# Wavelet mixer and gated feed-forward: sums of x and beta ahead of the weights, weights behind 1/den, the wait for zero pads at its reader

## The reference

```python
for _ in range(2):                                    # two analysis levels
    l = dwconv(low, h_filter)[:, ::2]
    h = dwconv(low, g_filter)[:, ::2]
    highs.append(h); low = l
low = linear_attention(low, 16)                       # q = k = elu(x) + 1, v = x, num / den
for h, L in zip(reversed(highs), reversed(lens)):     # two synthesis levels
    low = dwconv(repeat(low, 2), h_synth) + dwconv(repeat(h, 2), g_synth)
x = layernorm(x + (layer_norm(x + low) * gamma + beta))
gate, up = x @ wg.T, x @ wu.T                         # hidden width 1536, weights are integers / 127
x = layernorm(x + (silu(gate) * up) @ wd.T)
```

## Time and profile before

| | us |
|---|---|
| median of 3 runs | 1240.98 |
| lowest and highest | 1240.42, 1242.96 |
| the profiled execution | 1242.78 |
| its span | 1241.0 |

### The profile page before, as it was taken

One profiled execution on the slowest core, in us unless ns is written; L12 is line 12 of the kernel. 1 busy time (PEld: TensorE's weight loads), 2 busy tenths in 40 slices (PEclk: granted clock), 3 DMA queues, 4 the chain that ended last, 5 costly groups with the idle time before them and its releaser, 6 DMA issues.

```text
span 1241.0 us, 18461 instructions
## 1 busy us (share of the span) xinstructions
PE 1200.7 (97%) x5936; PEld 629.8 (51%) x5936; DVE 983.6 (79%) x1917; ACT 674.4 (54%) x1395; POOL 381.7 (31%) x794
## 2 busy tenths in 40 slices
PE   7968799999999999999999999999999999999997
PEld 6857454444544454444544544454445454454443
DVE  7968699998899989997799669965998579844231
ACT  5851474568545774567535653476355653565332
POOL 0013443146230652145221533044313522152201
PEclk9998899999999999999999999999999999999999
DMA  6794341203202221213102121212120210010000
GB/s 225 233 239 77 114 143 35 102 26 134 89 18 94 69 85 36 102 35 111 44 12 100 60 61 35 94 51 69 34 102 19 93 43 18 26 60 1 9 26 34
DMA packets 51864, 91.79 MB, mean 74 GB/s; under 512 B 8896, under 2 KB 28608, under 8 KB 50880
## 3 DMA queue, kind: packets, MB, share of 16 engines
q1 hardware_dynamic: 50048, 86.01, 21.3%
q0 software_dynamic: 1728, 4.72, 2.0%
HBM read 65.99 MB, written 25.19 MB: 73 GB/s over the span
## 4 chain that ended last, share of the span: by engine, by line
PE 81%; DVE 3%; POOL 3%; ACT 2%; issue 2%; POOLq 0%; DVEq 0%; ACTq 0%
PE ps_up L610 13%; PE ps_up L611 12%; PE ps_gate L610 12%; PE ps_gate L611 12%; PE ps_down L629 12%; PE ps_down L628 12%; PE ps_y L593 2%; PE ps_x L575 2%; PE ps_x L554 1%; PE ps_down L779 1%; POOL rs L1138 1%; DVE h L1211 1%; DVE l L1211 0%; DVE h_f L1599 0%; PE ps_x L534 0%
## 5 line engine op out<-in xcount | busy, mean ns | idle before, releaser
L610 PE MATMUL ps_gate<-x_hi,w 128*128 128x512 f16 x768 | 292.0, 380 | 1.6 <-DVE x_lo L1392 1.6
L610 PE MATMUL ps_up<-x_hi,w 128*128 128x512 f16 x768 | 291.9, 380 | 0.8 <-DVE h_f L1599 0.8
L611 PE MATMUL ps_gate<-x_lo,w 128*128 128x512 f16 x768 | 292.1, 380 | 0.0
L611 PE MATMUL ps_up<-x_lo,w 128*128 128x512 f16 x768 | 291.7, 380 | 0.0
L629 PE MATMUL ps_down<-w,hid 128*128 128x512 f16 x768 | 291.1, 379 | 0.0
L628 PE MATMUL ps_down<-w,hid 128*128 128x512 f16 x768 | 291.1, 379 | 0.0
L1076 ACT ACTIVATE h_f<-ps_gate 128x512 f32<-128x512 f32 x192 | 113.8, 593 | 212.3 <-PE ps_gate L611 212.3
L1599 DVE SCALAR_TENSOR_TENSOR h_f<-ps_up,h_f 128x512 f32<-128x512 f32 x192 | 130.7, 687 | 114.6 <-PE ps_up L611 105.0
L1586 DVE TENSOR_TENSOR hid<-h_f,hid 128x512 f16<-128x512 f32 x192 | 138.0, 719 | 2.8 <-ACT hid L1068 1.4
L1068 ACT ACTIVATE hid<-h_f 128x512 f16<-128x512 f32 x192 | 119.7, 624 | 34.7 <-DVE h_f L1599 34.3
L610 PEld LDWEIGHTS ps_up<-x_hi,w 128*128 128x128 f16 x768 | 75.3, 98 | 93.3 <-DVE h_f L1599 2.5
(11 more groups left out here) (239 smaller groups left out, 1733.7 us busy)
## 6 DMA issues: line engine op xcount, KB each, us to landing
xt<-x_tok SPq DMA_DIRECT2D x64, 256.0 KB, 2.6
out<-x SPq DMA_DIRECT2D x64, 256.0 KB, 2.1
xa<-x_chan SPq DMA_DIRECT2D x28, 515.0 KB, 5.2
xb<-x_chan SPq DMA_DIRECT2D x7, 2060.0 KB, 8.1
w<-weights POOLq DMA_DIRECT2D x12, 384.0 KB, 11.6
att<-den SPq DMA_DIRECT2D x32, 129.5 KB, 2.7
q_in<-q_scratch SPq DMA_DIRECT2D x7, 518.0 KB, 4.2
h_in<-h_scratch SPq DMA_DIRECT2D x7, 518.0 KB, 5.2
```

What stands on the lines that cost most here:

```text
L610: pe.matmul(ps_gu[k % 2][g][:, :], w, x1_hi[:, b, c, :], start=(c == 0), stop=False)
L611: mm = pe.matmul(ps_gu[k % 2][g][:, :], w, x1_lo[:, b, c, :], start=False, stop=(c == NC - 1))
```

## The change

Three edits. On GpSimd, the four sums of x and beta stand ahead of the weights, and the weights are issued after a wait for `ld_att[1]`, the semaphore of the last of the four copies of 1/den. On SP, the wait for the pads leaves the end of the opening and stands in `load_bands`, ahead of the waits that are there already. In the changed kernel the lines behind 410 have numbers one higher up to the place where the old wait was.

```diff
             def load_bands(j, batch):
                 at = (j - PER_BATCH * batch) * M2
 
+                hold(sp, zero_pads, 64)
                 hold(sp, st_q, 16 * PER_BATCH * (batch + 1))
...
             for t in range(DSUB):
                 after_norm2(0, 0, t)
-            hold(sp, zero_pads, 64)
...
             hold(pool, pro_conv1, 10)
-            load_weights(0, PIECES)
             pool.wait_ge(ld_const, 80)
             for t in range(DSUB):
                 xbeta(0, 0, t)
+            hold(pool, ld_att[1], 16)
+            load_weights(0, PIECES)
             for name, t in CLOSE_POOL:
```

## The result

The changed kernel takes 1229.18 us (median of 4 runs, 1227.76 to 1233.02) against 1240.9 us: a ratio of 0.9907, with a 95% interval of 0.9881 to 0.9933, 11.7 us less. In a second set of runs it took 1228.52 us (6 runs) against 1241.7, a ratio of 0.9905 (0.9887 to 0.9923). The ratios are those on record, estimated with their intervals from all runs of both kernels; they are not exactly the quotients of the medians. The forecast was 1231.0 us, 10.0 us less, with a range of 1226.5 to 1236.5. The profiled execution is the fastest of the first four, 1227.76 us.

What follows compares the result with a forecast made beforehand. TensorE, busy 1200.7 of 1241.0 us, bounds the kernel, so the first gate product's start at 145.33 decides. 9.3 us up to the norm's first turn plus 0.7 behind it give 10.0 less: 1231.0 us, range 1226.5 to 1236.5.

Steps and rivals of the forecast that it cites:

- The wait for 1/den: Close of the opening: last copy of 1/den lands at 83, with bounds of 81.2 and 97 (as now).
- The sums of x and beta: GpSimd's four sums, from 77.8 to 83.0, still cost VectorE 5.5 us, only earlier; att product at 88.8 instead of 95.21.
- The third rival: Beside the sums GpSimd gives way, not VectorE; att product at 83.3, gain of 12 to 15 us, 1227.5; chance 0.15.
- TensorE as the next bound: Between att and the norm TensorE runs without a gap; first turn at 108.3 against 117.62, 9.3 us earlier.
- the two cases of the clock: Clock falls to half in TensorE's idle time or not, one in two; first turn at 109.35 or 107.25.
- the sum for VectorE alone: From att to the last sum of the first half, gain on VectorE alone: 11.9 us.
- From there to the gate product: Norm's first turn to gate product: 0.7 us off GpSimd's 2.15 us step (bounds 0 and 1.6), clock unchanged.
- The weights: Issued from about 83.5 instead of 71.01; GpSimd free at 104.2 to 107.2, first mean due at 109.8; no cost.
- The zero pads: Their wait, moved to SP's loads of the bands, costs zero, with the loss bounded by 1 us.
- The total: Whole kernel: 9.3 + 0.7 = 10.0 us less, 1231.0 us against a median of 1240.98.
- The signs named ahead: Trace signs including copies landing in 3 to 7 us, a 5 to 6 us VectorE tap, gate product at 134 to 137.

Runs made afterwards that it cites:

- dose3: Changed kernel with three of the twelve weight pieces issued ahead of the sums of x and beta; 1234.66 us, 0.9943 of the kernel before.
- packed: Changed kernel with all four x tiles waited for ahead of the first sum of x and beta; 1231.77 us, 0.9924 of the kernel before.
- gaps: Changed kernel with the sums between the seventh and eighth weight pieces and two satisfied waits ahead of each sum; 1228.66 us, 0.9898 of the kernel before.
- beside_xb: Changed kernel with the sums of x and beta also waiting for VectorE's second att product; 1231.75 us in a single run.
- pads_only: Kernel before with only the wait for the zero pads moved to the loads of the bands; 1241.89 us, 1.0002 of the kernel before.
- seven: Changed kernel with the sums of x and beta between the seventh and eighth weight pieces; 1228.80 us, 0.9900 of the kernel before.
- sums_first: Changed kernel without the wait for the last copy of 1/den, sums still ahead of the weights; 1230.61 us, 0.9908 of the kernel before.

## Why the prediction was right, point by point

- **The wait for 1/den: right.** The queue was named as the cause and its own bandwidth as the measure. Expected was the last landing at 83; issued at 77.5 and landed 5.7 us later, it came at 83.2. dose3 shows the cause by its dose.
- **The sums of x and beta: the size was off.** I took the 5.5 us that they cost VectorE before. They cost 3.4 us in three turns. The att product, expected at 88.8, came at 86.00. Of these 2.8 us the sums are 2.1; the other 0.6 to 0.7 are chance: VectorE was already 0.6 us ahead in this trace before the first sum (`kv_blocks` at 78.11, at 78.71 in the trace before, and at 78.61 in another trace of the changed kernel, whose att product came at 86.49). The doubt stood in the prediction: the page "SBUF — State Buffer" of the Trainium skill says in its section "Who interferes with whom" that only a port pair which VectorE and GpSimd share causes contention, and that it is an exclusive lock. The trace of the changed kernel agrees with a lock that changes hands after each instruction (rows of 1.51 us beside sums of 1.3 to 1.6); the trace of before, with one VectorE row over four sums, does not, and packed, gaps and beside_xb narrow down the condition. The third rival thus came true in part: VectorE's turns, but not GpSimd giving way altogether.
- **TensorE as the next bound: right.** It ran without a gap from 86.47 to the first turn at 106.00, 20.0 us behind the att product; the two cases of the clock were 20.55 and 18.45. The clock did fall, 2.3 us into its idle time this time and for 3.4 us only. VectorE waited for it at 98.33, as the sum for VectorE alone (11.9 us) being larger than for TensorE (9.3) says. The first turn came 11.6 us earlier instead of 9.3: 2.8 us more from the att product, 0.5 less because TensorE took 20.0 us and not the mean of 19.5.
- **From there to the gate product: the size was off.** I gave 0.7 us; it was 2.4 (25.3 us instead of 27.7). Up to the convolutions of the second half it was 7.9 us instead of 9.0, for which GpSimd's small step, 1.5 us shorter and near the end of its bound, is enough. The runs agree with the reason forecast for it: the step took 2.15 us in each of the four kernels where it started beside VectorE's five taps (before, pads_only, seven and gaps), and 0.67 in all others. First two rows of before, then the same two of seven, then VectorE's row in the changed kernel:

```profile
120.60 2.15 POOL L1122 TENSOR_SCALAR rs<-rs 128x1 f32<-128x1 f32 x1 [1.02 <-ACT junk L866]
120.64 1.40 DVE L1211 SCALAR_TENSOR_TENSOR hid<-att,coef,hid 128x128 f32<-128x128 f32 x5
...
108.31 2.15 POOL L1122 TENSOR_SCALAR rs<-rs 128x1 f32<-128x1 f32 x1 [1.02 <-ACT junk L866]
108.36 1.39 DVE L1213 SCALAR_TENSOR_TENSOR hid<-att,coef,hid 128x128 f32<-128x128 f32 x5
...
109.17 0.75 DVE L1370 SCALAR_TENSOR_TENSOR x<-x,rs,gamma_b 128x512 f32<-128x512 f32 x1 [0.93 <-ACT junk L866]
```

  So seven and gaps pay for their earlier att product with a VectorE row of 5 us and with this step. The rest of the stretch, 1.2 us, goes with the clock: the convolutions at 113.88 took 1.53 us for six products; in the trace before they took 2.42, and the clock fell to half in them:

```profile
126.66 2.42 PE L779 MATMUL ps_down<-h,h_f 128*128 128x256 f32 x6 [3.05 <-ACT hid L894]
```

  I had left this stretch unchanged and had not counted it. Behind the gate product the clock rose after 3 us instead of 5.7, which is about the last us of the 15.0.
- **The weights: right, with less room.** They started at 85.61 (83.5), because the first x tile landed at 79.9 and not at 77.7 and the sums took 5.7 us instead of 5.2; eighth piece 103.28, GpSimd free at 105.9 (104.2 to 107.2). The spare time was 1.5 us and not 3 to 5, because the norm came 2.4 us earlier than I had it.
- **The zero pads: right**, nothing.
- **The total.** 10.0 forecast; 15.0 between the two profiled executions, 11.7 and 13.2 between medians. The two mis-sized terms have the same sign, the last us behind the gate product comes on top, and the profiled execution of the changed kernel is from the fast end of its eleven times, that of the kernel before (1242.78) from the slow end of its own. So the mechanism was right in the main, and that the median came within 2 us of 1231.0 is in part luck: the terms, as the traces have them, add up to 15 us and not 10.
- **The signs named ahead.** Four of the six came: the landing of the copies, no gap ahead of the att product, TensorE without a gap, the eighth piece at 103.28. Two did not: no tap of 5 to 6 us stood between 77 and 84 (the longest was 1.51 us, the sign of the third rival), and the gate product came at 131.32, ahead of 134 to 137.

## What to carry to other kernels

Two queues share the time of the same DMA engines: when something small and urgent lands in 19 us instead of 3, look at what the other queue was given just before, and price it by the dose (here 1.8 us for 384 KB). A transfer that is needed much later may start as late as its issuing engine allows, and that engine's next due step is the limit: here seven pieces fit and the eighth issue blocks GpSimd until the seventh has landed, so twelve pieces cost it 20 us. Before adding a wait, see what the order does already: the wait for 1/den was redundant once the sums stood first (sums_first), as long as the x tiles land behind 79.

## What the runs showed of the hardware

- The eighth piece of the weights was issued 0.3 to 0.4 us after the seventh had landed: at 103.28 (seventh issued at about 89.0 and 13.9 us to landing), and at 96.06 in the kernel before.
- Four sums of two SBUF operands on GpSimd, 5 us together, cost VectorE 4.5 to 5.5 us in one instruction directly behind DMA issues whose transfers were still under way, and 3.1 to 4.1 us in several where GpSimd had waited for something else.
- With TensorE's work in the same order, the stretches of the clock at half speed shifted from kernel to kernel by several us and were worth some 1 to 3 us each (an estimate: 22.3 against 20.0 us up to the first turn in dose3, 19.1 against 17.4 from the convolutions to the gate product in packed). They came in or behind TensorE's idle times of the close, also short ones: in packed the clock fell at 115.8, behind an idle time of 1.94 us; in the changed kernel it stayed high behind one of 1.95 us at the same place. Differences of this size between medians can't be given to an edit without a trace.
